# Input transposes, scaling and split moved to the end of the preceding slot, in a one-core attention and feed-forward kernel

## What is computed

```python
h = _layernorm(x) * (1 + ca) + sa
q, k, v = _rope(h @ Wq), _rope(h @ Wk), h @ Wv        # 16 heads of 32
ck, cv = 64 blocks of 16 tokens, each a weighted sum of k (of v)
out_comp = softmax(q ck^T, masked) cv
out_sel  = softmax(q k_sel^T, masked) v_sel           # the first 8 tokens of the 2 best blocks
out_win  = softmax(q k^T within the last 128 tokens) v
x = x + ga * ((g0 * out_comp + g1 * out_sel + g2 * out_win) @ Wo + bo)
h = _layernorm(x) * (1 + cb) + sb
x = x + gb * (h @ base_W^T + base_b + shared low-rank part + top-2-of-6 routed low-rank part)
```

## Time and profile before

| What | Value |
|---|---|
| median of 3 runs | 2372.66 us (2369.42 to 2372.81) |
| the profiled execution | 2375.0 us, of which its span 2373.1 us |
| mean granted TensorE clock | 0.962 |
| busy: PE, DVE, ACT, POOL | 90%, 74%, 56%, 33% of the span |
| one pass of the loop | 280.0 us, seven times |
| prologue, epilogue | 187.4 us, 227.9 us |

### The profile page before, as it was taken

The page is one execution under the profiler, slowest core; times in us unless marked ns, Lnnn a source line. Parts: engine busy times, 40 slices in busy tenths (PEclk is TensorE's granted clock), DMA queues, the critical chain, the costliest instruction groups (busy, mean ns, idle before and its releaser), DMA issues.

```text
span 2373.1 us, 48974 instructions
## 1 busy us (share of the span) xinstructions
PE 2145.7 (90%) x17944; PEld 1427.3 (60%) x17944; DVE 1749.7 (74%) x4740; ACT 1340.7 (56%) x4701; POOL 788.2 (33%) x780
## 2 busy tenths in 40 slices
PE   4888999899998999989999899989999899997887
PEld 0665666566665666656665566656666566664454
DVE  3456888768886788768887688866887678875776
ACT  1244666556665566646656566655666556663664
POOL 0333333343333233333332433324333423333221
PEclk9998999999999999989999899999999999997989
DMA  6010000200011000110001100020001100011000
GB/s 233 19 40 15 23 28 24 68 22 28 28 32 63 28 24 28 46 49 19 28 28 41 54 28 24 23 76 24 22 25 45 50 28 28 24 46 45 19 19 19
DMA packets 48892, 89.64 MB, mean 38 GB/s; under 512 B 6760, under 2 KB 6760, under 8 KB 48656
## 3 DMA queue, kind: packets, MB, share of 16 engines
q1 hardware_dynamic: 39440, 69.74, 9.6%
q10 hardware_dynamic: 9216, 16.78, 1.9%
HBM read 69.68 MB, written 16.83 MB: 36 GB/s over the span
## 4 chain that ended last, share of the span: by engine, by line
PE 63%; DVE 22%; ACT 6%; issue 5%; POOL 2%; DMA 1%; SPq 0%; DVEq 0%; ACTq 0%; POOLq 0%
PE ps_m L702 9%; PE ps_o L634 7%; PE ps_m L506 6%; PE ps_m L667 5%; PE ps_m L507 5%; PE ps_m L508 5%; PE ps_s L628 4%; PE ps_t L610 4%; DVE ps_s L1548 4%; ACT pw L1033 3%; PE ps_m L684 3%; DVE wmax L1553 3%; PE ps_s L597 3%; PE ps_s L586 3%; PE ps_m L705 2%
## 5 line engine op out<-in xcount | busy, mean ns | idle before, releaser
L1033 ACT ACTIVATE pw<-ps_s,wmax 128x128 f32<-128x128 f32 x1024 | 360.3, 382 | 168.5 <-DVE wmax L1553 168.4
L506 PE MATMUL ps_m<-w_hi,h_hi 128*128 128x512 f32 x768 | 374.0, 487 | 35.1 <-DVE rbf L1520 18.9
L1043 ACT ACTIVATE pw<-pw,wden 128x128 f32<-128x128 f32 x1024 | 313.2, 401 | 5.0 <-DVE wden L1563 4.8
L507 PE MATMUL ps_m<-w_lo,h_hi 128*128 128x512 f32 x768 | 309.7, 403 | 0.0
L508 PE MATMUL ps_m<-w_hi,h_lo 128*128 128x512 f32 x768 | 308.5, 402 | 0.0
L1067 ACT ACTIVATE pT<-ps_s 80x512 f32<-80x512 f32 (+7 forms) x240 | 141.9, 591 | 255.6 <-PE ps_o L634 155.7
L1311 POOL TENSOR_TENSOR h_lo<-hT,h_hi 128x512 fp32r<-128x512 f32 x57 | 72.3, 1268 | 540.4 <-ACT h_hi L993 540.4
L702 PE MATMUL ps_m<-wbt_s,h2T 128*128 128x512 f32 x512 | 249.0, 604 | 0.0
L667 PE MATMUL ps_m<-wo_s,aT 128*128 128x512 f32 x512 | 247.8, 609 | 0.0
L1574 DVE COPY_PREDICATED pT<-keep_prev,ps_t 128x512 f32<-128x512 uint32 x224 | 164.3, 733 | 94.2 <-PE ps_t L610 90.2
L1033 ACT ACTIVATION_READ_ACCUMULATOR pw<-ps_s,wmax 128x1 f32 x1024 | 226.6, 221 | 0.0
(11 more groups left out here) (187 smaller groups left out, 4341.9 us busy)
## 6 DMA issues: line engine op xcount, KB each, us to landing
xa<-x_in SPq DMA_DIRECT2D x65, 256.0 KB, 3.0
xc<-x_in SPq DMA_DIRECT2D x64, 256.0 KB, 2.8
out<-t ACTq DMA_DIRECT2D x64, 256.0 KB, 2.0
wo_s<-wo_in SPq DMA_DIRECT2D x8, 1024.0 KB, 6.3
wbt_s<-wbt_in SPq DMA_DIRECT2D x8, 1024.0 KB
gbc<-gate_rows SPq DMA_DIRECT2D x24, 256.0 KB, 5.4
pw<-wmod_in SPq DMA_DIRECT2D x3, 1024.0 KB, 5.5
pT<-wmod_in SPq DMA_DIRECT2D x3, 1024.0 KB, 5.3
```

Of the source, the lines that this page charges most:

```text
L506: pe_.matmul(ps[:], h_hi[:, c, :], w_hi[:, col, c, :], start=(c == 0), stop=False)
L507: pe_.matmul(ps[:], h_hi[:, c, :], w_lo[:, col, c, :], start=False, stop=False)
L1033: ins = act.activation(pw[:, hw, :], ps_w[:, j, i, 1, :], ACT.Exp, bias=wmax[:, hw:hw + 1], accum_out=wden[:, 0, hw:hw + 1])
L1043: act.activation(pw[:, hw, :], pw[:, hw, :], ACT.Copy, scale=wden[:, 2, hw:hw + 1]).then_inc(wn_ok, 1)
```

## The change

1. `transpose_h`, `h_scaled` and the split for tile t + 1 now stand near the end of the slot of tile t; for the first tile of a batch they are at the end of `turn`, with the low half on DVE. The ACT split waits until Q, K and V of tile t have been computed.
2. `t_spare` is true only for t > 0: all four groups of tile 0's compressed probabilities go through ps_t, one at a time. One wait of `cs_scores(1)` goes.
3. All slot orders of PE, ACT, POOL and DVE, and the banks, are rewritten. `mod_a` is copied earlier, in the new `next_mod`.

SyncE's list is not changed. The diff, cut to its core:

```diff
-FIRST_ORDER = [("HT", 0), ("Q", 1), ("K", 0), ("QT", 1), ("Y", 1), ("G", 0),
-               ("KT", 1), ("H2T", 0), ("Z", 0), ("F", 0), ("ZT", 1), ("V", 1)]
+FIRST_ORDER = [("Q", 0), ("K", 1), ("QT", 0), ("G", 1), ("Y", 0), ("KT", 0),
+               ("H2T", 0), ("Z", 1), ("F", 0), ("ZT", 1), ("V", 1), ("HT", 0)]
...
+SLOT_ORDER = [("Y", 1), ("Q", 0), ("K", 1), ("QT", 0), ("G", 0), ("H2T", 0),
+              ("Z", 1), ("F", 0), ("KT", 1), ("ZT", 1), ("V", 1), ("HT", 0)]
-TURN_ORDER = [("Y", 0), ("HT", 1), ("Q", 1), ("K", 0), ("V", 1), ("QT", 0),
-              ("KT", 0), ("H2T", 0), ("Z", 1), ("G", 0), ("F", 1), ("ZT", 0)]
+TURN_ORDER = [("Y", 1), ("Q", 0), ("K", 0), ("V", 1), ("QT", 0), ("KT", 0),
+              ("H2T", 0), ("G", 1), ("Z", 0), ("F", 0), ("ZT", 1), ("HT", 1)]
...
 def t_spare(t, g):
-    return t > 0 or g % 2 == 0
+    return t > 0
...
# PE, first_slot, as it now begins
+                window_scores(b, 1, 0)
+                project(seg, b, t, "Q", 0, [0, 1, 2, 3])
+                project(seg, b, t, "K", 1, [0])
+                window_scores(b, 1, 1)
+                project(seg, b, t, "K", 1, [1])
+                transpose_cs(b, 0, 0)
+                project(seg, b, t, "K", 1, [2])
+                cs_values(b, 0, 0)
+                transpose_cs(b, 0, 1)
+                project(seg, b, t, "K", 1, [3])
+                transpose_rot(seg, b, t, Ta, "QT", ra, 1)
+                cs_scores(b, 1)
+                transpose_cs(b, 0, 2)
...
# PE, slot
                 cs_scores(b, s)
-                transpose_h(seg, b, t, Ta)
                 output(seg, b, t, [0])
                 window_scores(b, s, 0)
-                output(seg, b, t, [1, 2, 3])
-                project(seg, b, t, "Q", 0, [0, 1, 2, 3])
+                output(seg, b, t, [1])
+                project(seg, b, t, "Q", 0, [0])
+                output(seg, b, t, [2, 3])
+                project(seg, b, t, "Q", 0, [1, 2, 3])
                 window_scores(b, s, 1)
...
+                project(seg, b, t, "V", 2, [0, 1])
+                transpose_h(seg, b, t + 1, Ta + 1)
                 cs_values(b, s, 2)
                 window_values(b, s, 3)
                 cs_values(b, s, 3)
-                project(seg, b, t, "V", 2, [3])
+                project(seg, b, t, "V", 2, [2, 3])
...
# PE, turn: its first part and its end as they now are
+                window_scores(ba, 0, 0)
+                output(seg, b, t, [0, 1])
+                project(seg, b, t, "Q", 0, [0, 1, 2, 3])
+                output(seg, b, t, [2])
+                project(seg, b, t, "K", 1, [0])
+                window_scores(ba, 0, 1)
+                project(seg, b, t, "K", 1, [1, 2, 3])
+                transpose_window(ba, 0, 0)
+                output(seg, b, t, [3])
+                project(seg, b, t, "V", 2, [0, 1])
...
+                transpose_h(seg, b, t + 1, Ta + 1)
+                feed(seg, b, t, [NC])
+                cs_scores(ba, 0)
+                window_values(ba, 0, 3)
...
# PE, end_first: begins window_scores(b, 1, 0), transpose_cs(b, 0, 0), window_scores(b, 1, 1)
# ACT, first_slot, as it now begins
+                cs_exps(b, 0)
+                window_exp(b, 1, 0)
+                window_norm(b, 1, 0)
+                probs_copy(b, 0, 0)
+                window_exp(b, 1, 1)
...
# ACT, head
                 h_scaled(seg, b, t + 1, "HT", hT, mod_a, moda_ok, 1)
-                copy_v(seg, b, t)
+                gate_exp(t)
                 split_h(seg, b, t + 1, t + 1, t)
-                gate_exp(t)
                 copy_qT(seg, b, t)
                 copy_kT(seg, b, t)
+                copy_v(seg, b, t)
...
# ACT, slot: the end as it now is
+                h_scaled(seg, b, t + 1, "HT", hT, mod_a, moda_ok, ba + 1)
                 copy_out(b, s)
+                copy_v(seg, b, t)
+                split_h(seg, b, t + 1, Ta + 1, t)
                 store(seg, b, t)
...
# POOL, first_slot, whole
+                residual_in(b, t)
                 cs_normalise(b, 0)
                 rotate(seg, b, t, Ta, "Q", ra)
-                residual_in(b, t)
                 scale_feed(b)
+                cs_subtract(b, 1)
+                cs_normalise(b, 1)
                 rotate(seg, b, t, Ta, "K", kr)
-                cs_subtract(b, 1)
                 deviation_c(NT * b + t)
                 weigh_keys(seg, b, t, Ta)
-                cs_normalise(b, 1)
                 deviation_a(Ta + 1)
+                split_h(Ta + 1)
...
# POOL, end_first: residual_in now first there too. POOL, turn: scale_out before cs_subtract
# DVE, turn: the end as it now is
+                split_probs(ba, 0, 3)
+                final(seg, b, t)
                 cs_mask(ba, 0)
                 cs_max(ba, 0)
+                split_low(Ta + 1)
```

More of the change, by code:

```diff
@@ L727, in first_slot @@
-                project(seg, b, t, "K", 1, [2])
                 cs_values(b, 0, 3)
-                cs_scores(b, 1)
-                project(seg, b, t, "K", 1, [3])
                 transpose_window(b, 1, 0)
-                output(seg, b, t, [0, 1, 2, 3])
-                gate_logits(seg, b, t, [0, 1, 2, 3])
+                output(seg, b, t, [0, 1, 2])
+                transpose_window(b, 1, 1)
+                output(seg, b, t, [3])
+                window_values(b, 1, 0)
+                transpose_cs(b, 1, 0)
@@ L734, in first_slot @@
+                gate_logits(seg, b, t, [2, 3])
+                transpose_window(b, 1, 2)
+                transpose_cs(b, 1, 1)
                 transpose_rot(seg, b, t, Ta, "KT", kr, 2)
-                window_values(b, 1, 0)
+                cs_values(b, 1, 0)
+                window_values(b, 1, 1)
                 transpose_h2(seg, b, t)
-                transpose_window(b, 1, 1)
+                transpose_cs(b, 1, 2)
+                cs_values(b, 1, 1)
+                window_values(b, 1, 2)
@@ L899, in end_first @@
                 window_values(b, 1, 2)
-                feed(seg, b, t, [NC])
-                transpose_cs(b, 1, 3)
+                transpose_h2(seg, b, t)
                 cs_values(b, 1, 2)
@@ L904, in end_first @@
                 cs_values(b, 1, 3)
+                lora_down(seg, b, t)
+                feed(seg, b, t, [0, 1, 2, 3])
+                transpose_z(seg, b, t)
+                feed(seg, b, t, [NC])
             def end_slot(seg, b, s):
@@ L927, in end_slot @@
                 transpose_window(b, s, 3)
-                transpose_z(seg, b, t)
-                transpose_cs(b, s, 3)
                 cs_values(b, s, 1)
@@ L932, in end_slot @@
                 cs_values(b, s, 2)
+                transpose_cs(b, s, 3)
+                feed(seg, b, t, [NC])
                 window_values(b, s, 3)
                 cs_values(b, s, 3)
-                feed(seg, b, t, [NC])
             def last(seg, b):
@@ L1120, in slot @@
                 Ta = NT * ba + t
-                h_scaled(seg, b, t, "HT", hT, mod_a, moda_ok, ba + 1)
-                split_h(seg, b, t, Ta)
                 window_exp(b, s, 0)
@@ L1129, in slot @@
                 probs_copy(b, s, 0)
+                window_norm(b, s, 1)
+                copy_z(seg, b, t)
                 gate_exp(Ta)
-                copy_z(seg, b, t)
                 router_exp(b, t)
@@ L1166, in turn @@
                     copy_zT(seg, b, t)
+                h_scaled(seg, b, t + 1, "HT", hT, mod_a, moda_ok, ba + 2)
+                if c2:
                     store(seg, b, t)
+                split_h(seg, b, t + 1, Ta + 1, t)
             def head(t):
@@ L1738, in first_slot @@
                 window_max(b, 1, 0)
+                rope(seg, b, t, "Q")
                 window_weights(b, 1, 0)
-                split_low(Ta)
+                cs_factor(b, 0)
                 window_max(b, 1, 1)
-                cs_factor(b, 0)
-                rope(seg, b, t, "Q")
+                rope(seg, b, t, "K")
                 cs_mask(b, 1)
                 cs_max(b, 1)
-                rope(seg, b, t, "K")
+                window_weights(b, 1, 1)
                 split_probs(b, 1, 0)
+                cs_factor(b, 1)
+                split_probs(b, 1, 1)
                 residual(seg, b, t)
@@ L1848, in end_first @@
                 window_max(b, 1, 1)
+                cs_mask(b, 1)
+                cs_max(b, 1)
+                split_probs(b, 1, 0)
+                cs_factor(b, 1)
+                split_probs(b, 1, 1)
                 window_weights(b, 1, 1)
-                cs_mask(b, 1)
-                split_probs(b, 1, 0)
-                cs_max(b, 1)
+                split_probs(b, 1, 2)
                 residual(seg, b, t)
                 ln_scale(x1[:], mvc, vec, xc[:, t % 2, :], lnc, lncp, NT * b + t)
-                cs_factor(b, 1)
-                split_probs(b, 1, 1)
+                split_probs(b, 1, 3)
                 router(seg, b, t, 0)
                 router(seg, b, t, 1)
-                split_probs(b, 1, 2)
-                split_probs(b, 1, 3)
                 final(seg, b, t)
```

279 lines of the change are left out of this document (125 added, 154 removed).

## The result

The changed kernel took **2446.55 us** (median of 4 runs, 2442.87 to 2446.79), the kernel before 2372.73 beside it: a ratio of **1.0307** (95% interval 1.0289 to 1.0325). The forecast was 2384, range 2345 to 2408. The direction was right; the time lies 39 us above the range.

A forecast was written before the change was run, and what follows sets the result against it. TensorE held 63% of the chain of waits, with most loss in first_slot. Terms -3.5 - 9.8 + 9.9 + 10.5 + 3.8 = +10.9 on 2375.0 gave 2385.9, less 2.3 to the median: 2384 us, range 2345 to 2408.

The forecast's parts named there:

- Heads: Prologue's seven heads: ACT splits h without copying V first, 0.5 us off each, -3.5 us.
- Boundary behind the prologue: From cs_scores(0) to the next slot, xc loaded long before: 41.1 us against 50.86, -9.8 us.
- the walk: Instruction lists followed behind cs_scores(0) after the prologue: 35.8 us of work plus 5.3 of waits, 41.1 in all.
- The six others: Later batch boundaries: POOL waits for xc, PE waits 8.4 us at transpose_cs; +1.65 us each, +9.9 in all.
- C: Start of cs_scores(0) in turn, forecast 34.8 us behind turn's start.
- The first rival: POOL's first instruction in first_slot isn't held because xc lands early: -53.7 us, 2319; chance 0.15.
- the hold: In first_slot POOL's residual_in waits for xc, everything compressed behind it; xc lands 16.3 us behind F's end.
- Slots: Slots of each pass: later transposes cost time, fewer switches save some; +1.5 us a pass, +10.5 in all.
- putting HT behind: Next tile's transposes at the slot's end: costs 0.45 us from slot 4 on, 0.1 to 0.3 in slots 2 and 3.
- fewer switches: PE's rear part of each slot loses 0.2 us less a slot.
- Epilogue: In end_first, PE idles before transpose_cs behind the same late load: 85.9 us against 82.13, +3.8.
- The third rival: Clock flickers or the slots' tails wait: 0.5 us more in each of 42 slots, 2405; chance 0.1.

The follow-up runs named there:

- Experiment 7: Next batch's first xc load issued before the weight reloads: changed kernel 2403.20 us, kernel before 2373.15; instead, residual_in later on POOL in the changed kernel: 2421.80.
- experiment 1: Changed kernel with weigh_keys put back behind deviation_a on POOL in the plain slots: 2414.29 us.
- experiment 2: Kernel before with only weigh_keys moved ahead of the next tile's power on POOL in the plain slots: 2402.04 us.
- experiment 6: Changed kernel with the earlier kernel's plain-slot order, next tile's transposes kept at slot end: 2414.31 us; with V's copy ahead of the scaling and xc early: 2371.52.

## Why the prediction was right or wrong

- **Heads: wrong, -3.5 became +3.1.** The wait of the earlier trace rows fell from 1.77 to 0.82 us, but the new order brought 0.36 for K's rotate, and more switches: PE is busy 11.26 us a head for 10.80. A head takes 12.48 us against 12.57, a gain of 0.1 instead of 0.5. The loss is elsewhere: the heads begin 2.1 us later, the first two take 1.3 and 1.5 more (the second at a mean clock of 0.88 for 1.00), and the rest gave 1.7 back. How much of it is the change's is open: in nine other kernels with this very prologue `cs_scores(0)` comes at 183.4 to 187.2 us, in the three with the old one at 182.9 to 183.8. The rows of the changed kernel:

```profile
95.00 0.63 PE L517 MATMUL ps_m<-cst,kr 128*128 128x128 f32 x4 [0.36 <-POOL kr L1282]
...
96.44 0.47 PE L506 MATMUL ps_s<-w_hi,h_hi 128*128 128x512 f32 x1 [0.82 <-POOL h_lo L1318]
```

- **Boundary behind the prologue: right**, 41.51 for 41.1. Its waits were 0.39, 0.40, 1.46, 1.14 and 0.64 for the 0.6, 0.4, 1.3, 1.3 and 0.6 of the walk, and the clock stayed at 1.00. That the sum is so close is partly luck: the waits came to 4.6 for 5.3, and PE was busy 36.9 us for 35.8.
- **The six others: right in mechanism.** First `transpose_cs` at C + 18.68 (forecast 18.65), wait 8.06 (8.4), C at 35.10 behind `turn`'s start (34.8). V in `turn` waited 1.1 us for DVE's x (1.3). The clock cost was mis-sized: 49.48 - 41.51 - (8.06 - 1.14) = 1.05 us for the 2.6 taken. The first rival, POOL isn't held, is refuted by the trace (12.26 us of waiting for xc). Experiment 7 gives the price of the hold: 43 us, where the prediction had 65 between its forecast of 2384 and this rival's 2319. Without the hold a boundary still takes 42.8 to 44.2 us behind `cs_scores(0)`, not the 41.1 of the walk.
- **Slots: this step failed.** "`transpose_z` has 0.1 us to spare; a miss may cost 0.3 a slot" became a wait of 0.77 in each of 42 slots, and "+1.5 a pass" became +9.25. The walk moved every instruction with its old duration, and the prediction doesn't name `weigh_keys` at all: it did not ask what VectorE would be doing when POOL came to that step. The copy of the indices went from 0.17 to 1.23 us. By experiment 1 that is 0.84 us a slot, 34 us in the passes, about half of the 65; experiment 2 shows it in the kernel before. The other terms of the slots were mis-sized. That putting HT behind costs 0.45 was right in kind: 0.7 (experiment 6). That taking it out in front gains nothing held in slots 4 and 5, but not in 2, 3 and 6. And the 0.2 that "fewer switches" should have saved in the rear became a loss of 0.3 to 0.7 by the rest of the new order, whose cause is only in part seen. The sum itself was off too: 0.45 in four slots and 0.1 to 0.3 in two, less 0.2 in each of six, give 0.8 to 1.2 a pass, not 1.5.
- **Epilogue: right in sign.** +6.6 up to its slot 2 for +3.8; what follows gave 1.1 back. That part is luck: its slots 2 to 6 ran at a higher clock than before and took 3.9 us less (last section).
- **The third rival** had the right place in one half (the slots' tails) and 0.1 of the chance; its 0.5 us on top of the forecast's own 0.25 a slot are half of the 1.54 measured. Its other half, the clock, is refuted: the changed kernel's slots 2 to 7 ran at 1.00 in the pass shown.

## What to carry to other kernels

When instructions change places on one engine, look up what the other engine of the shared pair runs at that moment: rows of the kernel before already show the price (xa at 1.48 us instead of 0.55), one only has to ask who would pay it next. Look for the stretch that another engine bounds, and move a step into it, not out of it. And an in-order list that waits for a transfer should have only what needs that transfer behind it: the hold went from xc to wb_s to `deviation_c` before a split of the long step resolved it.
